# Moving the first row's tap products to GpSimd and the mask's steps ahead in a fused four-layer convolution block

## What is computed

```python
x = x + _L0_conv_ref(_gn(x), ...)   # whitening over channels, by power iteration
x = x + _L1_conv_ref(_gn(x), ...)   # deformable 3 x 3 convolution, 16 groups of 8 channels
x = x + _L2_conv_ref(_gn(x), ...)   # attention in 7 x 7 windows, then among the window tokens
x = x + _L3_conv_ref(_gn(x), ...)   # masked 3 x 3 convolution
```

```python
offset = x1 @ off_w + off_b
mask = jax.nn.softmax((x1 @ mask_w + mask_b).reshape(N, H, W, G, P), -1)
# per tap: bilinear sample of xproj at the pixel + tap + offset, times mask; sum over the nine taps
samp = (v00 * (1 - wx) + v01 * wx) * (1 - wy) + (v10 * (1 - wx) + v11 * wx) * wy
return jnp.einsum('hwpc,hwp->hwc', samp, m)
```

## Time and profile before

| | us |
|---|---|
| median of three runs | 9815.72 |
| lowest and highest run | 9799.69, 9819.58 |
| the profiled execution | 9807.95 |
| its span, first to last instruction | 9806.1 |
| busy in it: TensorE, VectorE, ScalarE, GpSimd | 8025.1, 7400.9, 3946.4, 191.2 |

### The profile page before, as it was taken

One profiled execution on the slowest core, in us unless ns is written; L12 is line 12 of the kernel. 1 busy time (PEld: TensorE's weight loads), 2 busy tenths in 40 slices (PEclk: granted clock), 3 DMA queues, 4 the chain that ended last, 5 costly groups with the idle time before them and its releaser, 6 DMA issues.

```text
span 9806.1 us, 288571 instructions
## 1 busy us (share of the span) xinstructions
PE 8025.1 (82%) x123582; PEld 4502.0 (46%) x123582; DVE 7400.9 (75%) x8865; ACT 3946.4 (40%) x6124; POOL 191.2 (2%) x253
## 2 busy tenths in 40 slices
PE   6458888887888888798888878888887988888797
PEld 5324445354444545444453534445353444535354
DVE  2478778868777886878788687878868787886863
ACT  0034435354343535434353533435353343535332
POOL 0000000000000000000000000000000000000000
PEclk7579999998999999899999989999998999999898
DMA  4000201111020111112011111201111110111101
GB/s 116 0 20 22 58 23 48 31 46 42 28 59 23 48 31 46 42 30 58 23 48 30 47 42 32 59 21 47 31 47 42 31 57 22 47 31 46 42 26 53
DMA packets 231836, 391.50 MB, mean 40 GB/s; under 512 B 26736, under 2 KB 168016, under 8 KB 223312
## 3 DMA queue, kind: packets, MB, share of 16 engines
q1 hardware_dynamic: 230544, 372.67, 13.5%
HBM read 190.38 MB, written 130.55 MB: 33 GB/s over the span
## 4 chain that ended last, share of the span: by engine, by line
PE 58%; DVE 23%; issue 12%; ACT 6%; DVEq 1%; DMA 0%; SPq 0%; POOL 0%; ACTq 0%; POOLq 0%
PE ps L895 11%; PE ps L694 8%; PE ps L760 7%; DVE arena L1720 5%; PE ps L995 4%; PE ps L793 4%; PE ps L985 3%; PE ps L809 3%; PE ps L768 3%; DVE arena L1775 3%; PE ps L716 3%; PE ps L782 2%; DVE arena L1697 2%; DVE arena L1815 1%; DVE arena L1703 1%
## 5 line engine op out<-in xcount | busy, mean ns | idle before, releaser
L895 PE MATMUL ps<-arena,ident 64*64 64x512 f32 x5600 | 1752.1, 679 | 650.3 <-DVE arena L1720 650.1
L897 PE MATMUL ps<-arena,ident 48*64 48x512 f32 x5600 | 1756.0, 680 | 0.0
L1720 DVE TENSOR_TENSOR arena<-arena 112x2560 f32<-112x2560 f32 x560 | 1578.1, 2819 | 95.8 <-PE ps L897 89.3
L895 PEld LDWEIGHTS ps<-arena,ident 64*64 64x64 f32 x5600 | 490.2, 148 | 1686.8 <-issue 1678.0
L760 PE MATMUL ps<-arena,wqk 128*128 128x400 f32 x2048 | 888.3, 551 | 156.1 <-DVE arena L1824 114.4
L694 PE MATMUL ps<-vp,convw 128*128 128x448 f32 x2016 | 822.8, 550 | 23.6 <-ACT vp L1316 23.6
L1703 DVE TENSOR_TENSOR arena<-arena 112x576 f32<-112x576 f32 x1008 | 764.2, 758 | 34.9
L809 PE MATMUL ps<-arena 64*64 64x33 f32 x32768 | 636.7, 226 | 118.5 <-issue 64.5
L1237 ACT ACTIVATE arena<-ps 112x864 f32<-112x864 f32 x224 | 199.2, 889 | 1273.1 <-PE ps L716 1268.4
L793 PE MATMUL ps<-ident,arena 128*128 128x128 f32 x4096 | 575.1, 285 | 142.6 <-ACT arena L1116 43.3
L1815 DVE TENSOR_REDUCE arena<-ps 128x16 f32<-128x800 f32 x512 | 504.9, 986 | 245.3 <-PE ps L782 241.6
(11 more groups left out here) (299 smaller groups left out, 12428.4 us busy)
## 6 DMA issues: line engine op xcount, KB each, us to landing
windows_out<-arena SPq DMA_DIRECT2D x1024, 100.0 KB
arena<-windows_out SPq DMA_DIRECT2D x224, 256.0 KB, 3.9
arena<-windows_out SPq DMA_DIRECT2D x224, 192.0 KB, 3.3
arena<-in_wqk SPq DMA_DIRECT2D x16, 2048.0 KB, 8.2
arena<-in_x_t SPq DMA_DIRECT2D x16, 1568.0 KB, 10.4
arena<-in_x SPq DMA_DIRECT2D x16, 1568.0 KB, 7.3
arena<-arena SPq DMA_DIRECT2D x32, 784.0 KB
out_x<-xb SPq DMA_DIRECT2D x112, 224.0 KB, 2.0
```

Of the source, the lines that this page charges most:

```text
L895: nc.tensor.matmul(ps[half, 3, :], ident[0:SLOT, 0:SLOT], prod[0:SLOT, ring(c, dy), dx, :], start=(s < 2), stop=(s >= TAPS - 2), skip_grou ...
L897: mm = nc.tensor.matmul(ps[half, 4, :], ident[SLOT:PT, SLOT:], prod[SLOT:PT, ring(c, dy), dx, :], start=(s < 2), stop=(s >= TAPS - 2), ski ...
L1720: V.tensor_tensor(prod[0:PT, ring(c, dy), :, :].rearrange("p k (n e) -> p k n e", e=CG), taps.to_broadcast([PT, SHIFTS, N64, CG]), for_tap ...
```

## The change

Two things are done. First, for tiles 1 to 6 of each sample the product of `by_row` for the first tap row (bb = 0) is made by GpSimd, in `zero_taps`, behind the fill of that tile's weights; VectorE waits for it (`t_r`, "row_terms") and does the three additions as before. Tile 0 keeps its product on VectorE. `rw_s` is now counted up by the hats-times-mask instruction itself for these tiles, and GpSimd waits for it. Second, in VectorE's loop `sum_mask` and `norm_mask` of the next tile move from the end of slot 3 to the end of slot 2, and `rows_by_mask` from the end of slot 3 to ahead of the product of slot 3. The count of VectorE's own chain falls from 105 to 93 per sample.

```diff
--- before.py
+++ after.py
@@ -57,7 +57,7 @@
 ADD_Q = [min(at + 4, 2 * TR * SHIFTS - 7 + k) for k, at in enumerate(CONV_Q[2::3])]
 DVE_A, DVE_COV, DVE_POW = 20, 12, 22
 ACT_MAIN = 14
-DVE_PRE, DVE_MAIN, DVE_BLK, DVE_END = 6 + 8 * DW_BLOCKS, 105, 69, 46
+DVE_PRE, DVE_MAIN, DVE_BLK, DVE_END = 6 + 8 * DW_BLOCKS, 93, 69, 46
 
 
 
@@ -327,7 +327,7 @@
 
         of_p, of_c, of_h, ht_s = (sig(k, 2 * TR) for k in ("off_psum", "off_copied", "off_read", "hats"))
         ms_s, mk_e, rw_s = (sig(k, TR) for k in ("mask_shifted", "mask_exp", "mask_in_hats"))
-        k_z, k_s = sig("taps_zeroed", TR), sig("tap_rows_built", 3 * TR)
+        k_z, k_s, t_r = sig("taps_zeroed", TR), sig("tap_rows_built", 3 * TR), sig("row_terms", TR - 1)
         pr_s, pr_u = sig("prod_ready", SHIFTS * TR), sig("prod_used", SHIFTS * TR)
         sum_s, dc_p, dc_s, oo_p, rs_s = (sig(k, TR) for k in ("sum_sbuf", "sum_turned", "dc_sbuf", "out1_psum",
                                                               "res1_added"))
@@ -555,10 +555,16 @@
                         pool.wait_ge(s_p.sem, s_p.at(i, PAIRS if u else PAIRS - 4))
                         alone(pool)
                     nc.gpsimd.memset(kw[u][0:PT, :], 0.0).then_inc(k_z.sem, 1)
-                for c in range(2, TR):
-                    pool.wait_ge(pr_s.sem, pr_s.at(n, (c - 1) * SHIFTS))
+                for c in range(1, TR):
+                    if c >= 2:
+                        pool.wait_ge(pr_s.sem, pr_s.at(n, (c - 1) * SHIFTS))
+                        alone(pool)
+                        nc.gpsimd.memset(kw[c % 2][0:PT, :], 0.0).then_inc(k_z.sem, 1)
+                    pool.wait_ge(rw_s.sem, rw_s.at(n, c + 1))
                     alone(pool)
-                    nc.gpsimd.memset(kw[c % 2][0:PT, :], 0.0).then_inc(k_z.sem, 1)
+                    nc.gpsimd.tensor_tensor(
+                        terms[0:PT, :].rearrange("p (a n) -> p a n", a=3), hat_later[0:PT, :, 0, :],
+                        hat_later[0:PT, 0, 1:2, :].to_broadcast([PT, 3, HN]), ALU.mult).then_inc(t_r.sem, 1)
 
             def zero_windows(i):
                 pool.wait_ge(l1_s.sem, l1_s.at(i))
@@ -1682,20 +1688,26 @@
                 logits, hat = logits_of(c), offsets_of(c)[1]
                 dve.wait_ge(ht_s.sem, ht_s.at(n, 2 * c + 2))
                 ownm.settle()
-                ownm.mark(V.tensor_tensor(hat[0:PT, :, 1, :], hat[0:PT, :, 1, :],
-                                          logits.rearrange("p (a n) -> p a n", a=1).to_broadcast([PT, 3, HN]),
-                                          ALU.mult))
+                ins = V.tensor_tensor(hat[0:PT, :, 1, :], hat[0:PT, :, 1, :],
+                                      logits.rearrange("p (a n) -> p a n", a=1).to_broadcast([PT, 3, HN]), ALU.mult)
+                if c:
+                    ins.then_inc(rw_s.sem, 1)
+                else:
+                    ownm.mark(ins)
 
             def by_row(n, c, bb):
 
                 tt, hat = terms if c else om_first, offsets_of(c)[1]
                 if bb:
                     dve.wait_ge(k_s.sem, k_s.at(n, 3 * c + bb))
-                else:
+                elif not c:
                     ownm.settle()
                     dve.sem_inc(rw_s.sem, 1)
-                ownm.step(V.tensor_tensor(tt[0:PT, :].rearrange("p (a n) -> p a n", a=3), hat[0:PT, :, 0, :],
-                                          hat[0:PT, bb, 1:2, :].to_broadcast([PT, 3, HN]), ALU.mult))
+                if c and not bb:
+                    dve.wait_ge(t_r.sem, t_r.at(n, c))
+                else:
+                    ownm.step(V.tensor_tensor(tt[0:PT, :].rearrange("p (a n) -> p a n", a=3), hat[0:PT, :, 0, :],
+                                              hat[0:PT, bb, 1:2, :].to_broadcast([PT, 3, HN]), ALU.mult))
                 if bb == 0:
                     dve.wait_ge(k_z.sem, k_z.at(n, c + 1))
                 for aa in range(3):
@@ -1972,6 +1984,8 @@
                     ahead = c + 1 < TR
                     for dy in range(SHIFTS):
                         s = c * SHIFTS + dy
+                        if ahead and dy == 3:
+                            rows_by_mask(n, c + 1)
                         multiply(n, c, dy)
                         if dy == 0:
                             by_row(n, c, 1 if c else 2)
@@ -1990,10 +2004,9 @@
                             far_flag(n)
                         if i is not None:
                             after_windows(i, 2 * s + 1)
-                        if ahead and dy == 3:
+                        if ahead and dy == 2:
                             sum_mask(n, c + 1)
                             norm_mask(n, c + 1)
-                            rows_by_mask(n, c + 1)
                         elif ahead and dy == 4:
                             by_row(n, c + 1, 0)
```

## The result

The changed kernel took 10064.86 us (median, 10054.8 to 10070.51), the kernel before beside it 9814.36 us: a ratio of 1.0253, 95% interval 1.0236 to 1.027, or 250 us more. The forecast was 9910 us with a range from 9830 to 10000 us; the sign was right and the size was not. The profiled execution has a span of 10061.4 us where before had 9806.1.

The account below looks back on a forecast made before the run. TensorE was taken to set each sample's end from the convolution's first matmul on. 0.5 + 4.44 + 2.3 - 0.2 = 7.0 us in 15 samples, less 8, gave + 97 us: 9905, put at 9910 us, range 9830 to 10000.

Parts of the forecast that it names:

- What bounds the kernel: Tiles stage: from the convolution's first matmul on, TensorE alone sets the sample's end; any delay of that point is paid in full.
- What is removed: 96 first-row tap products of 1950 ns leave VectorE: at most 187 us, if VectorE were last to arrive everywhere.
- GpSimd's product: The 96 added products of 112x1728 on GpSimd: 3.1 us each, between 1.55 and 4.64 us.
- Hidden: GpSimd's result is wanted 5.5 us after its start, so even 4.64 us costs nothing unless the engines hinder each other.
- The rival with 0.33: GpSimd's reading holds each tap product (c, 4) by 3.1 us: + 139 us, near 9950 us; chance 0.33.
- Tile 4: Mask steps ahead of (4, 3) delay the convolution 4.44 us, plus 2.3 for a low-clock sum, less 0.2, per later sample.
- What arrives at tile 4: Lateness from tiles 0 to 3: 2.9 us from tile 1 vanish in tile 3's 7.02 us wait; + 0.5 us, ends -1.9 and + 1.
- The first sample: No earlier sample to finish, so VectorE sets its pace: -1.2 us in five tiles, -1.9 in the first, together -8 us.
- The sum: 7.0 us a sample, 15 times, less 8 us for the first: + 97 us, 9905 us, put at 9910 us.
- small loss: Clock stays up at tile 4 and VectorE arrives 1.9 us early: + 27 us in all, near 9840 us; chance 0.13.
- faster: ScalarE's relu holds the convolution's first matmuls and covers the later product: -37 us, 9775 us; chance 0.14.

Follow-up runs that it names:

- e1_moves: The kernel before with only the mask's steps moved, the first tap row's product staying on VectorE: 9955.12 us, + 1.31%.
- e6: The changed kernel with GpSimd multiplying only half of the 1728 columns and filling the other half with zero: 9964.33 us.
- e3_fill: The changed kernel with GpSimd filling the 1728 places with zero instead of multiplying, so that it reads nothing: 9955.76 us.
- e4_tile4_old: The changed kernel with the mask's steps of tile 4 alone put back to the end of slot 3: 9977.58 us.

## Why the prediction was off, point by point

**What bounds the kernel.** Right. Behind L694 the time is the same within 0.2 us in before, after and e1 to e6, and in the later samples the loss arrives as a later L694.

**What is removed** was priced at up to 187 us and expected to bring nothing but the first sample. Right: e1_moves and e3_fill are 1 us apart.

**GpSimd's product** was sized at 3.1 us with bounds of 1.55 and 4.64. Its own time is 3.7 us, within the bounds; what the profile shows is 6.25 us, since the wait for VectorE counts in. "Hidden" was right for the row's additions, which never wait for it, and wrong for the tap product beside it. The rival with 0.33 was what happened. Its hold (3.1 us at each (c, 4)) was right to the tenth in tiles 1, 4 and 5, and too small in tile 0 (3.6) and too large in tiles 2 and 3 (1.8 and none). Its first sample was near: 2.5 us a tile over the forecast, measured 345.0 - 325.7 = 19.3 us over e3_fill, or 3.2 in each of six tiles. Wrong was what it passed on: 1.7 us a sample by tile 4, measured 7.1 (9.9 - 2.8 by tile) or 6.9 (233.7 - 226.8 by stage). That tiles 2 and 4 have the slack was right. But tile 1 passed on 3.7 us for its hold of 3.1, tile 0 passed on 1.7 us, and tile 3, whose wait of 7.02 us was to take it all up, added 2.1.

**Tile 4** was right: wait ahead of (4, 3) 5.23 us (5.2 forecast), clock 0.54, convolution behind it without a gap; 5.7 us by e4_tile4_old where 6.5 were reckoned.

**What arrives at tile 4** is the step that failed. The forecast said + 0.5, because the 2.9 us from tile 1 would end in tile 3's wait of 7.02 us. Measured in the mean of the later samples were + 9.9 us after the change and + 2.8 us without hindrance (e3_fill). Up to tile 2 the forecast was right: 2.9 us late in the mean (2.0 in the fourth sample). But the last sum of tile 3 ended 2.9 us late (4.1 in the fourth sample) instead of 0. Two of its assumptions fell. The second sum behind a low-clock one was priced at 2.8 us and took 3.8 in the mean (4.6 in the fourth sample). And the delays inside tiles 2 and 3 were left out, 1.0 us by the start of tile 3 in the mean: in the fourth sample a sum took 4.5 us (2372.82 to 2377.30; the matmuls ahead of it had waited 1.28 us for ScalarE) that had taken 2.8 us before. With hindrance the arrival was + 9.8 us in this sample. So of the 9.4 us between the + 0.5 and the + 9.9 measured, 7.1 are the hindrance, which the forecast's sum had put at nothing ("hidden"), and 2.3 are the moves' own.

**The first sample** was forecast at - 8 us; without hindrance it was - 4.9 (e3_fill), with it + 14.4.

**The sum.** Moves alone: 97 us forecast, 130 measured. Hindrance: 42 us over the forecast in its rival (139 against 97), some 119 measured. The hindrance as measured, on the forecast's own moves, gives 9910 + 119 = 10029 us and is past the range by itself; the 33 us of the moves make up the rest. By stage the same gap of 153 us (250 - 97) is 15 x (16.6 - 7.0) = 144 in the tiles, 22 in the first sample, and some 10 less in the windows stage, where 0.7 us a sample is no more than kernels differ there. The rivals *small loss* and *faster* stood on the clock staying up and on the relu being late, and the trace has neither.

## What to carry to other kernels

Before an elementwise step is moved to GpSimd, look at what VectorE runs beside it: where both read SBUF and VectorE read two operands, they took turns here, and the moved step cost VectorE up to its own length on GpSimd, which is longer than it was on VectorE (3.1 us of hold and 3.7 of length against 1.95 us). Work taken from an engine is worth nothing where that engine isn't the last to arrive; look for the step whose lateness is passed on (here the sum ahead of L694) and put things behind it. And when a delay of 3 us is said to be absorbed by a wait, price the work around the wait at the clock that it will find (3.8 us for a sum that was reckoned at 2.8), and add what the tiles ahead of it bring.

## What was not expected of the hardware

- The hold reaches small instructions. In tile 3 no tap product was held (2.80 us), but a 128 x 1 step of the group norm, which otherwise takes 0.22 us, stands in the trace with 1.83 us, up to the end of GpSimd's product; so it does in all 15 later samples, and never with the fill:

```profile
2462.24 1.83 DVE L1549 SCALAR_TENSOR_TENSOR sm<-sm 128x1 f32<-128x1 f32 x1
```
```profile
2457.79 6.26 POOL L565 TENSOR_TENSOR arena<-arena 112x1728 f32<-112x1728 f32 x1 [49.10 <-DVE arena L1691]
```

- Held time counts as busy time in both engines' totals: VectorE's busy time is 257 us more than with the fill (7480.8 against 7223.5), with the same number of instructions, and the two waits show in no list of waits.
- A GpSimd copy (one operand read) waits for a tap product and holds the next just as the product does, for 0.9 us; fills of 1600 and 1728 elements (1.43 and 1.54 us) never did either.
- Keeping TensorE's granted clock up in the tiles shortened them by 3.4 us a sample, and the windows stage behind them, which was not changed, was longer by 3.3. Whether the one brings the other is open.
